# Masks by DMA transposes, rows by transposes, and the first residual's bias by memory fill and adding stores

## The reference

```
x  = layernorm(x + gcn(x, W0, b0))
# layer 1: 4 heads of 256; xl = x @ W1; softmax over the edges of leaky_relu(alpha_src[src] + alpha_dst[dst])
h  = relu(layer_norm(gat(x, W1, a_src1, a_dst1, b1), g1, be1)) + (x @ Wr1 + br1)
# layer 2: one head of 768
y  = layer_norm(gat(h, W2, a_src2, a_dst2, b2), g2, be2) + (h @ Wr2 + br2)
out = layernorm(x + y)
```

## Time and profile before

| | us |
|---|---|
| median of 3 runs | 844.95 (844.8 to 847.12) |
| the profiled execution, whole | 844.18 |
| its span, first to last instruction | 842.3 |
| PE busy | 808.9 (96%) |
| DVE busy | 672.1 (80%) |
| ACT busy | 268.8 (32%) |
| POOL busy | 60.1 (7%) |
| DMA | 73.55 MB, 87 GB/s over the span |

### The profile page before, as it was taken

The page is one execution under the profiler, slowest core; times in us unless marked ns, Lnnn a source line. Parts: engine busy times, 40 slices in busy tenths (PEclk is TensorE's granted clock), DMA queues, the critical chain, the costliest instruction groups (busy, mean ns, idle before and its releaser), DMA issues.

```text
span 842.3 us, 13750 instructions
## 1 busy us (share of the span) xinstructions
PE 808.9 (96%) x5022; PEld 533.0 (63%) x5022; DVE 672.1 (80%) x1181; ACT 268.8 (32%) x510; POOL 60.1 (7%) x81
## 2 busy tenths in 40 slices
PE   5899998999999999999999998999999999999995
PEld 4577774665554444447888887886666666555553
DVE  7999995777676659999988879969872287996686
ACT  2454456010011201015555455643301107760000
POOL 3000002011103000000000000011110000001111
PEclk9999999999999999999999999999999999999998
DMA  8000004041131353235212104113223342112232
GB/s 306 7 2 2 2 3 170 25 162 57 45 156 70 100 178 124 82 120 201 61 59 86 53 1 138 57 63 126 88 63 94 124 137 76 65 57 75 75 113 71
DMA packets 24588, 73.55 MB, mean 87 GB/s; under 512 B 2756, under 2 KB 3756, under 8 KB 24398
## 3 DMA queue, kind: packets, MB, share of 16 engines
q1 hardware_dynamic: 23262, 67.61, 23.3%
q0 software_dynamic: 1264, 5.11, 1.8%
HBM read 52.40 MB, written 20.31 MB: 86 GB/s over the span
## 4 chain that ended last, share of the span: by engine, by line
PE 89%; DVE 5%; issue 3%; DVEq 2%; ACT 1%; DMA 0%; POOL 0%; SPq 0%; POOLq 0%
PE psum L957 19%; PE psum L984 19%; PE psum L750 18%; PE psum L1065 12%; PE psum L872 8%; PE psum L762 6%; PE psum L814 3%; PE psum L972 1%; PE psum L998 1%; DVEq L1359 1%; PE psum L909 1%; PE psum L937 1%; ACT arena L1072 1%; PE psum L807 1%; PE psum L723 1%
## 5 line engine op out<-in xcount | busy, mean ns | idle before, releaser
L984 PE MATMUL psum<-arena 128*128 128x257 f32 x800 | 175.4, 381 | 2.6 <-DVE arena L1601 1.6
L1072 ACT ACTIVATE arena<-psum 128x160 f16<-128x160 f32 (+6 forms) x188 | 93.4, 528 | 258.9 <-PE psum L750 74.8
L984 PEld LDWEIGHTS psum<-arena 128*128 128x128 f32 x800 | 151.2, 190 | 26.2 <-ACT arena L1072 2.7
L750 PE MATMUL psum<-arena 128*128 128x512 f16 x720 | 159.3, 379 | 2.3 <-DVE arena L1429 1.9
L957 PE MATMUL psum<-arena 128*128 128x512 f16 x960 | 158.5, 326 | 0.2 <-ACT arena L1072 0.2
L957 PEld LDWEIGHTS psum<-arena 128*128 128x128 f16 x960 | 93.5, 97 | 62.3 <-ACT arena L1072 0.5
L750 PEld LDWEIGHTS psum<-arena 128*128 128x128 f16 x720 | 69.3, 98 | 86.4 <-issue 7.0
L1065 PE MATMUL psum<-arena 128*128 128x512 f16 (+2 forms) x600 | 98.4, 326 | 0.0
L1065 PEld LDWEIGHTS psum<-arena 128*128 128x128 f16 x600 | 58.3, 97 | 39.8
L1457 DVE CUSTOM_DVE_ANT_0 arena<-arena 128x1280 bf16<-128x1280 bf16 x50 | 71.0, 1488 | 14.1 <-DMA arena<-as_scratch 8.2
L1175 ACT ACTIVATE arena<-arena 128x640 f32<-128x640 f32 x80 | 64.5, 836 | 49.4 <-DVE arena L1586 49.2
(11 more groups left out here) (173 smaller groups left out, 714.9 us busy)
## 6 DMA issues: line engine op xcount, KB each, us to landing
arena<-in_L_gnn_W_dram SPq DMA_DIRECT2D x22, 384.0 KB, 3.2
r_scratch<-arena SPq DMA_DIRECT2D x10, 512.0 KB, 2.6
arena<-uv_scratch SPq DMA_DIRECT2D x16, 320.0 KB, 4.4
arena<-r_scratch SPq DMA_DIRECT2D x10, 512.0 KB, 3.7
x_scratch<-arena SPq DMA_DIRECT2D x10, 384.0 KB, 4.5
arena<-x_scratch SPq DMA_DIRECT2D x10, 384.0 KB, 3.5
r_scratch<-arena SPq DMA_DIRECT2D x10, 384.0 KB, 2.6
arena<-r_scratch SPq DMA_DIRECT2D x10, 384.0 KB, 3.7
```

The source lines that it names most:

```text
L750: ins = pe.matmul(o[:, a:b], part[:, k, ds(t * P, P)], w[:, k, a:b], start=(not begun and k == 0 and n == 0 and m == 0), stop=(k == kn - 1 ...
L984: last = pe.matmul(p_att[:, ATT_BANKS[ch][j], 0:HID + 1], pf[n % PSLOTS][:, j * P:(j + 1) * P], xl[ch % H][:, k, 0:HID + 1], start=(k == 0 ...
L1072: act.activation(out_, in_, ACT.Copy, scale=scale).then_inc(signal, 1)
```

## The change

- **Masks.** PE's transposes of `c_hi` are gone. SP stores `c_hi` to DRAM (`c_scratch`, 3.28 MB) once it is complete, and after the last aggregation tile loads it back with ten DMA transposes, each a 128 x 1280 block of f16, into `c_turned`, which lies on the same bytes as `neg`. DVE makes the masks in place, from SBUF, after the evictions of xl 2 (four), 3 (three) and 4 (three); each waits for all ten DMAs. `X1_ORDER` is regular now, and tile 0's eviction no longer waits for tile 1.
- **Rows.** `rows_of` uses PE's transpose in place of an f32 matmul.
- **Bias of r1.** The two matmuls per tile, POOL's preparation of br1, and its load are gone. A DMA from DRAM to DRAM writes br1 into all 1280 rows of `r1_scratch` (5.24 MB) at the start of stage 2, ahead of W1's slabs, and each r1 tile is added to it by a store that accumulates. Such stores are issued by POOL, not SP.
- **Order on SP.** W1's slabs 3 to 5 come behind the store of `c_hi`; the store of `neg` comes between Wr1's slabs 1 and 2.

```
+MASKS_AT = {2: range(0, 4), 3: range(4, 7), 4: range(7, T)}
...
-            weights(1)
+            sp.wait_ge(S["w_hi"], KD)
+            sp.dma_start(r1_d.rearrange("t p n -> (t p) n"), br1.rearrange("(a n) -> a n", a=1).to_broadcast([T * P, HC])).then_inc(S["r1_fill"], 16)
+            weights(1, range(3))
+            sp.wait_ge(S["blk_free"], NB)
+            sp.dma_start(c_d, c_hi.rearrange("p t n -> p (t n)")).then_inc(S["c_out"], 16)
+            weights(1, range(3, KD))
             for t in range(T):
                 sp.wait_ge(S["x1_ok"], t + 1)
                 sp.dma_start(x1_d[t], x1_sb[:, t, :]).then_inc(S["x1_out"], 16)
+            sp.wait_ge(S["c_out"], 16)
+            sp.wait_ge(S["gcn_done"], T)
+            for k in range(T):
+                sp.dma_start_transpose(c_turned[:, :, k * P:(k + 1) * P], c_d[:, k * NP:(k + 1) * NP]).then_inc(S["c_turn"], 16)
+            sp.wait_ge(S["x1_out"], 16 * T)
+            sp.wait_ge(S["x1_tr"], T)
+            weights(2, range(2))
             sp.wait_ge(S["neg_ok"], T)
             sp.dma_start(neg_d, neg.rearrange("p t n -> p (t n)")).then_inc(S["neg_out"], 16)
-            sp.wait_ge(S["x1_out"], 16 * T)
-            sp.wait_ge(S["x1_tr"], T)
-            weights(2)
+            weights(2, range(2, KD))
...
-                sp.wait_ge(S["r1_read"], t + 1)
-                sp.dma_start(r1_d[t], r_st[t % 2]).then_inc(S[f"r1_out{t % 2}"], 16)
...
+            pool.wait_ge(S["r1_fill"], 16)
+            for t in range(T):
+                pool.wait_ge(S["r1_read"], t + 1)
+                pool.dma_start(r1_d[t], r_st[t % 2], accum_op=ALU.add).then_inc(S[f"r1_out{t % 2}"], 16)
...
-                for a in (0, 512):
-                    pe.matmul(o[:, a:a + 512], ones_row, br1_parts[:, a:a + 512], start=True, stop=False)
-                product(o, (x1t_hi, x1t_lo), (wr1_hi, wr1_lo), t, KD, HC, range(KD // 2), True)
+                product(o, (x1t_hi, x1t_lo), (wr1_hi, wr1_lo), t, KD, HC, range(KD // 2))
...
-                    last = pe.matmul(o[:, i * P:(i + 1) * P], column[:, t:t + 1].to_broadcast([P, P]), ident, start=True, stop=True)
+                    last = pe.transpose(o[:, i * P:(i + 1) * P], column[:, t:t + 1].to_broadcast([P, P]), ident)
...
-                dve.wait_ge(S["neg_tr"], t + 1)
-                dve.tensor_scalar(neg[:, t, :], p_neg[t % 2], 0.0, NEG_BIG, ALU.is_equal, ALU.mult).then_inc(S["neg_ok"], 1)
+                dve.wait_ge(S["c_turn"], 16 * T)
+                dve.tensor_scalar(neg[:, t, :], c_turned[:, t, :], 0.0, NEG_BIG, ALU.is_equal, ALU.mult).then_inc(S["neg_ok"], 1)
...
                     dve.wait_ge(S["xl_done"], t + 1)
                     project(t, H, HID, p_x[t % 2], a_junk)
-                    if t:
-                        xl_evict(t)
+                    if t == 0:
+                        dve.wait_ge(S["par_b1"], 16)
+                        dve.wait_ge(S["c_out"], 16)
+                    xl_evict(t)
+                    for m in MASKS_AT.get(t, ()):
+                        mask(m)
```

More of the change, by code:

```diff
@@ L351, in gnn_program @@
         r2_d = nc.dram_tensor("r2_scratch", [T, P, D], f32).ap()
+        c_d = nc.dram_tensor("c_scratch", [P, T * NP], f16).ap()
         neg_d = nc.dram_tensor("neg_scratch", [P, T * NP], bf16).ap()
@@ L405, in step_count @@
             return steps_done, enter_loop, leave_loop
-        X1_ORDER = [("tr", 0), ("tr", 1)]
-        X1_ORDER += [s for k in range(KD) for s in [("part", 0, k)] + ([("neg", k - 3)] if k >= 3 else [])] + [("xl", 0)]
-        X1_ORDER += [s for k in range(KD) for s in [("part", 1, k)] + [[("neg", 3)], [("tr", 2)], [("neg", 4), ("tr", 3)], [("neg", 5), ("neg", 6)], [("neg", 7)], [("neg", 8), ("neg", 9)]][k]] + [("xl", 1)]
+        X1_ORDER = [("tr", 0), ("tr", 1)] + [("part", 0, k) for k in range(KD)] + [("tr", 2), ("xl", 0)]
+        X1_ORDER += [("part", 1, k) for k in range(KD)] + [("tr", 3), ("xl", 1)]
         X1_ORDER += [s for i in range(2, T) for s in [("tr", t) for t in (2 * i, 2 * i + 1) if t < T] + [("xl", i)]]
@@ L647, in _ @@
                 pool.memset(pair[:, :, :, HID:HID + 2], 1.0).then_inc(S["xl_ones"], 1)
[L648 to L657, removed]
             param("par_a2s", a_src2.rearrange(flat), 3, D)
@@ L750, in product @@
                                 ins = pe.matmul(o[:, a:b], part[:, k, ds(t * P, P)], w[:, k, a:b],
-                                                start=(not begun and k == 0 and n == 0 and m == 0), stop=(k == kn - 1 and n == 1))
+                                                start=(k == 0 and n == 0 and m == 0), stop=(k == kn - 1 and n == 1))
                 return ins
@@ L890, in slot_read @@
             def slot_read(t, last):
-                if last and last[0] == "neg":
-                    pe.wait_ge(S["neg_ok"], last[1] + 1)
-                elif last:
+                if last:
                     pe.wait_ge(S["x1t_lo_ok"], last[1] + 3)
@@ L904, in _ @@
                     last.then_inc(S["x1_tr"], 1)
[L905 to L910, removed]
                     used[t % 2] = (what, t)
@@ L1485, in _ @@
                     x1t_low(t)
-                elif what == "neg":
-                    mask(t)
                 elif what == "xl":
-                    if t == 1:
-                        dve.wait_ge(S["par_b1"], 16)
-                        xl_evict(0)
                     dve.wait_ge(S["xl_done"], t + 1)
                     project(t, H, HID, p_x[t % 2], a_junk)
-                    if t:
-                        xl_evict(t)
+                    if t == 0:
[4 more added lines that the diff above has]
+                        mask(m)
                     weights(2, WR1_AT.get(t, ()))
```

28 lines of the change are left out of this document (9 added, 19 removed).

## The result

| | before | after |
|---|---|---|
| median, us | 846.0 (844.8 to 847.12) | 834.79 (834.19 to 838.65) |
| the profiled execution, whole | 844.18 | 838.65 |
| its span | 842.3 | 836.8 |
| PE busy | 808.9 | 797.3 |
| DMA, MB | 73.55 | 84.81 |

The ratio of the times is 0.9878, 95% interval 0.9848 to 0.9907. The forecast was 834.0. Both medians are of four runs; that of before, 846.0, stands 1.05 above the 844.95 that the forecast was made from. The profiled execution of after is the slowest of its four (the others took 834.2 to 835.0), so it has to be read with care; a second profile of the same kernel, `after_again`, stands beside it.

The account below looks back on a forecast made before the run. PE, busy 808.9 of 842.3 us, was taken as the bound. 844.18 - 7.1 (masks) - 0.5 (bias) - 3.3 (rows) = 833.3 profiled, 834.0 as median; forecast 831 to 838, wider range 831 to 852.

Parts of the forecast that it names:

- the signs that the prediction named: Traces to check; wrong if W1 slabs land after 164 or attention starts over 1 us off 83.8 after xl 9's end.
- Masks: xl stage: mask transposes off PE gain 7.1 us, xl 9 ending near 292.4; each mask on DVE takes 0.64.
- tr 5's new wait: xl stage: tr 5 shares tr 3's PSUM slot and comes right after tr 3 and 4, so PE waits 1.2 us.
- DMA transposes: Before the masks: ten take 18 us (bounds 9.0 and 68), landed at 230, needed by 240.7, so no cost.
- rival (a): DMA transposes land after 240.7, each microsecond late lost; gain gone at 40 us (82 GB/s), 873 at worst; 28 in 100.
- The fill: Aggregation stage: writing br1 to r1_scratch takes 14.4 us and costs 0; half pace (29 us) would cost 1 or less.
- c_hi's store: Aggregation stage: takes 9.0 us, needed by DVE at 221, has 60 us, costs 0.
- Adding stores: r1 stage: each takes 8 us, three times the plain store's 2.6; free up to 13.9.
- Bias: r1 stage: 6.4 us of matmuls off PE, 0.5 gained, as DVE is 0.2 to 0.3 us behind PE.
- only DMA landing times in it could, and none is touched: r1 stage: DVE's 84 us will not shrink, against keeping the bias gain in full (828 us, 3 in 100).
- rival (d): After PE's 5 us wait in r1 the clock drops, costing at most 1.75 us: 835.8; 15 in 100.
- Rows: Groups of ten in rows_of: transposes take 1.09 us in place of 2.23, three groups, 3.3 us gained.

Follow-up runs that it names:

- masks_rows: The changed kernel without its bias part: bias matmuls and plain r1 stores are back, masks and rows stay changed; 835.89 us, ratio to before 0.9892.
- double_turn: The changed kernel with the ten DMA transposes issued twice, the second set after the first has landed, masks waiting for both; 852.85 us, ratio 1.0081.
- plain_turn: The changed kernel with ten plain loads of the same bytes in place of the DMA transposes, so counts are not turned; 835.99 us, ratio 0.9884.
- bias_only: The kernel before with only the bias part (fill, adding stores, no bias matmuls); masks and rows as before; 847.18 us, ratio 1.002.
- rows_only: The kernel before with only the transposes in rows_of in place of matmuls; 842.82 us, ratio 0.9967.
- head0_after: The changed kernel with head 0's row spread by ten PE transposes and two ACT copies, not through DRAM; 834.69 us, ratio 0.987.
- head0_cut: head0_after with uv's transpose after 6 of tile 8's 36 matmuls instead of 18; 832.1 us, ratio 0.9843.

## Why the prediction was right, and where it was not

**The sum.** It takes 10.9 off. The terms as measured (6.9, 3.3, and -0.9 for the bias) make 9.3, and that is what the second group of runs shows: 846.15 - 836.65 = 9.5. The first shows 11.2. So the closeness of 834.0 to 834.79 is in part luck. The medians of the changed kernel themselves move by nearly 2 between the groups (834.79, 836.65), and the term for the bias was off by 1.4 with no other to make up for it. By the signs that the prediction named, too, it was partly wrong: slabs of W1 came after 164, and PE reached attention 87.3 after xl 9's end (87.1 in `after_again`), not 83.8.

**Masks: right.** Predicted 7.1, with xl 9 ending at 292.4. It ended at 292.35 in `after_again` (whose xl began 0.36 early) and 292.7 in `masks_rows`, 6.9 less from xl's first matmul; in after, late and at half clock in the first tile, at 294.7. tr 5's new wait was 1.33, forecast 1.2. The mask was 0.42, not 0.64: a row of half the length on other operands was too dear a neighbour, and it didn't matter.

**DMA transposes: right that they are free, the landing mis-sized.** I took 18 us. SP alone needed 23.2 to issue the ten, and the last landed near 237: 26 us after 211.3, 127 GB/s, as the first set of `double_turn` did in 25.8. The margin to the masks was 4.6, not 11. The Trainium skill (DMA: Bandwidth & Descriptors, Latency and other measured facts) has 261 GB/s for such a transpose; here it was half that, and the trace decides. My bounds of 9 and 68 held it. For rival (a) I set 82 GB/s against a row at over four times that pace, but that row is one store; ten plain loads ran at some 157 GB/s (an estimate, from the 21 us of `plain_turn`), under twice the 82.

**The fill: its time mis-sized, its price right but for the clock.** 14.4 was taken, 31.1 measured (169 GB/s; 29.1 to 30.1 in the others), worse than the half pace of 29. DVE waited 5.33 for W1. I had given half pace a price of 1 or less. PE lost 0.7 in that execution and nothing in the others, but the longer idle (2.61 for 1.94) was followed by 1.7 of half clock, which the prediction had not priced here. The cover was some 4.7, not the 5.4 that I took. c_hi's store, taken at 9.0, landed 35.9 after its issue at 142.13, behind the fill, still well before 221.

**Adding stores: right.** Forecast 8, 5.5 landed; ACT never waited for one. But I asked only who waits for them, not what they travel with.

**Bias: the sign of the term was wrong.** Forecast 0.5 gained; measured 1.0 lost (`bias_only`), 0.8 (`masks_rows` against `after_again`). The step that held: DVE is just behind PE, so PE's 6.4 turn into idle time before uv's transpose (forecast 5, measured 5.1 to 6.9 in six profiles). The steps that failed are two. First, "only DMA landing times in it could, and none is touched". From the issue of the `as_scratch` store to the first maximum it took 8.3, 8.6 and 10.1 in the profiles without the bias part (before, `masks_rows`, `rows_only`), and 8.9 to 11.3 in the eight with it that keep this trip. The means are 1.3 apart, but the ranges overlap, and the 84.3 that I started from held the shortest trip of all (8.3), so part of the miss is the base. Whether the adding stores or something else in the queues does the rest, no run told apart. Second, rival (d), half clock behind the wait, is real: 54 matmuls took 13.73 for 11.65. That is 2.1, above the 1.75 that I took for the most. It is hidden as long as DVE is later still, as in `after_again`. The Trainium skill (TensorE: Matmul & The Clock Gate, Part 1) has TensorE fall from 2.4 to 1.2 GHz when it is found idle; the windows here agree (0.50 from 368 to 372).

**Rows: right.** Forecast 3.3, 3.3 in `rows_only`. In the chain of after a group is 1.09, the value I worked out; the earlier trace rows has 2.23.

**The range.** 831 to 852 held it. Its upper end rested on rival (a), which `double_turn` shows at 852.85 with the transposes issued twice.

## What to carry to other kernels

Work taken off the engine that bounds a stage counts only up to the path just behind it, so measure that one as closely (here DVE, 0.2 us behind, through two trips to DRAM) and shorten it first. A trip through DRAM on such a path varied by 2 us here with nothing changed in it (8.3 and 10.1), and the two longest parts of one (a store of 7.4, loads of 8.6) each had a store of 512 KB issued less than half a microsecond ahead; that the store was the cause is not shown. To call two paths level from one execution is to read noise. And an idle gap that replaces the work can cost clock behind it, once even where it was only 0.7 longer than before (2.61 for 1.94).

## What the runs showed of the hardware

- After an idle PE of 5.1 to 6.9 us the granted clock was 0.5 (1.2 of 2.4 GHz) for 3 to 5 us. After 2.61 it was 0.53 to 0.62 for 4 us, and after 2.29 0.70 as a mean of 5 us; after 2.39 and 2.65 (`head0_after`, `head0_cut`) attention began at 0.66 to 0.67 (375 to 380). After 1.94 (before, `after_again`) and 1.73 (`masks_rows`) it stayed at 1.00.
- A DMA transpose of a 128 x 1280 f16 block keeps SP for 1.9 us (median, 1.4 to 5.5) and lands 5.0 after its issue (after); a plain load of the same 320 KB landed 5.6 after its issue (`plain_turn`). Ten of the first took 25.8 (`double_turn`), ten of the second some 21 (an estimate from the median landing).
- A DMA from DRAM to DRAM that repeats one row 1280 times ran at 169 GB/s, the store of 3.28 MB from SBUF of the earlier trace rows at 364.
- An adding store of 512 KB landed in 5.5 us, the plain one in 2.6.
